# Query projections of one head and four tiles in the first attention layer of a fused transformer kernel

## The reference

```
q = (latents @ Wq).reshape(b, q_len, N_KV_HEADS, N_GROUPS, HEAD_DIM)      # 16 x 64 rows, 32 heads of 128
k = (hidden_states @ Wk)...   v = (hidden_states @ Wv)...                # context and latents, 4 kv heads
scores = einsum('bqhgd,bkhd->bhgqk', q, k) / sqrt(HEAD_DIM)               # 64 x 128 per head
out = softmax(scores) @ v ;  return out @ Wo                             # then x = x + out, layer norm
```

## Time and profile before

| what | value |
|---|---|
| median of three runs | 1513.99 us |
| profiled execution: time, span of its instructions | 1514.85 us, 1513.1 us |
| mean granted TensorE clock | 0.992 |
| PE, PEld, DVE, ACT, POOL busy | 97%, 87%, 68%, 61%, 27% |
| first attention | about 12 to 625 us of the span |

### The profile page before, as it was taken

One profiled execution on the slowest core, in us unless ns is written; L12 is line 12 of the kernel. 1 busy time (PEld: TensorE's weight loads), 2 busy tenths in 40 slices (PEclk: granted clock), 3 DMA queues, 4 the chain that ended last, 5 costly groups with the idle time before them and its releaser, 6 DMA issues.

```text
span 1513.1 us, 27936 instructions
## 1 busy us (share of the span) xinstructions
PE 1472.1 (97%) x9532; PEld 1316.5 (87%) x9532; DVE 1032.4 (68%) x2449; ACT 926.9 (61%) x3133; POOL 402.4 (27%) x461
## 2 busy tenths in 40 slices
PE   8999999999999999998999999999999999989997
PEld 7999999999999998887888888888888888877885
DVE  7556555655565557886777777777777788767776
ACT  4456455545564555547777777777777774466652
POOL 5112011301130102233232323232323242644431
PEclk9999999999999999999999999999999999989999
DMA  5000100010000100101111110101010101011101
GB/s 219 33 29 29 43 29 29 29 43 29 29 29 29 43 29 27 57 35 43 36 43 42 37 50 29 50 29 50 29 50 29 39 8 67 29 46 37 48 15 60
DMA packets 16115, 62.60 MB, mean 41 GB/s; under 512 B 2228, under 2 KB 3764, under 8 KB 10984
## 3 DMA queue, kind: packets, MB, share of 16 engines
q1 hardware_dynamic: 15976, 60.82, 11.5%
HBM read 58.72 MB, written 2.10 MB: 40 GB/s over the span
## 4 chain that ended last, share of the span: by engine, by line
PE 54%; issue 26%; DVE 9%; ACT 6%; POOL 4%; DMA 0%; SPq 0%; POOLq 0%; ACTq 0%; DVEq 0%
PE psY L958 12%; PE psQ L874 9%; PE psKV L898 7%; PE psSO L843 2%; PE psSO L945 2%; POOL wo L541 2%; PE psTP L859 2%; PE psTP L908 2%; PE psQ L859 1%; PE psQ L799 1%; PE psSO L844 1%; PE psTP L928 1%; PE psKV L814 1%; ACT prob L1487 1%; PE psQ L1245 1%
## 5 line engine op out<-in xcount | busy, mean ns | idle before, releaser
L958 PE MATMUL psY<-wo,oT 128*128 128x512 f32 x1536 | 378.2, 394 | 0.7 <-DVE oT L1943 0.2
L958 PEld LDWEIGHTS psY<-wo,oT 128*128 128x128 f32 x1536 | 278.8, 188 | 56.2 <-POOL wo L541 2.2
L541 POOL TENSOR_TENSOR wo<-stage_o,wo 128x512 fp32r<-128x512 f32 x68 | 87.2, 1313 | 310.3 <-ACT wo L1400 279.6
L1400 ACT ACTIVATE pT<-psTP 64x256 fp32r<-64x256 f32 (+1 forms) x192 | 86.5, 451 | 124.2 <-PE psTP L928 123.4
L1490 ACT ACTIVATE prob<-wide,neg_mx 128x128 f32<-128x128 f32 x256 | 99.7, 391 | 81.5 <-DVE neg_mx L2075 81.5
L1487 ACT ACTIVATE prob<-s_sb,neg_mx 128x64 f32<-128x64 f32 x256 | 85.9, 337 | 94.2 <-DVE neg_mx L2075 94.2
L1943 DVE TENSOR_TENSOR pT<-psTP,pT 64x256 fp32r<-64x256 f32 (+1 forms) x192 | 97.6, 508 | 67.3 <-ACT pT L1400 65.5
L665 POOL TENSOR_TENSOR rms<-ms_eps,minus_half 128x5 f32<-128x5 f32 (+1 forms) x64 | 74.2, 1159 | 230.6 <-DVE ms_eps L2088 229.8
L541 POOL TENSOR_TENSOR wq<-stage_q,wq 128x512 fp32r<-128x512 f32 x42 | 53.9, 1301 | 209.3 <-ACT wq L1400 156.6
L898 PEld LDWEIGHTS psKV<-wkv,arena 128*128 128x128 f32 x768 | 100.3, 190 | 6.8 <-DVE kT L2123 1.8
L874 PE MATMUL psQ<-wq,hT 128*128 128x512 f32 x384 | 103.8, 407 | 0.0
(11 more groups left out here) (329 smaller groups left out, 3489.9 us busy)
## 6 DMA issues: line engine op xcount, KB each, us to landing
stage_o<-in_wo SPq DMA_DIRECT2D x16, 1024.0 KB, 4.8
stage_q<-in_wq SPq DMA_DIRECT2D x15, 1024.0 KB, 5.1
stage_kv<-in_wkv SPq DMA_DIRECT2D x12, 512.0 KB, 3.6
stage_q<-in_ctx SPq DMA_DIRECT2D x16, 256.0 KB, 3.0
stage_o<-in_ctxT SPq DMA_DIRECT2D x2, 1024.0 KB, 4.8
stage_q<-in_base SPq DMA_DIRECT2D x2, 1024.0 KB, 4.9
stage_kv<-in_ctx SPq DMA_DIRECT2D x8, 256.0 KB, 3.0
out<-x_res SPq DMA_DIRECT2D x8, 256.0 KB, 2.2
```

The lines of the kernel that those rows point to most:

```text
L541: g.tensor_tensor(dst[LO], stage, dst[HI].bitcast(f32), ALU.subtract).then_inc(ld[done or what + "_lo"], 1)
L958: m = mm(psY[:], oT[:, ol, h, :], wo[:, wl, h, :], start=h == 0 and i == 0, stop=h == HQ - 1 and i == 2)
L1400: copy = lambda o, i: nc.scalar.activation(o, i, ACT.Copy)
```

## The change

In head groups 1 to 6 a unit is one head for four tiles: 4 slices x 3 passes = 12 matmuls of 512 columns (`lat_four`). Groups 0 and 7 keep the units of two heads and two tiles. A query buffer `heads_of_four` of 16 KB per partition takes the place of kT1, v1, qT and xn; it holds four tiles' heads and is refilled in place. Its upper end is shared with xn, so that some norms (`alone`) go to q_sb, a single buffer. PE computes units earlier: unit t + 3 in step t, reached by two units each in steps 4 and 6; no unit stands in steps 53 and 54. ACT and DVE copy two units in every even step of groups 1 to 6, one before `exps` / `normalise` and one after, and none in odd steps. The splits of Wq move to steps 5, 12, 20, ..., 52, those of Wk and Wv to 14, 30 and 46. `ln_norm` of the next block goes behind `row_max` in steps 60 to 62.

```diff
+    at_top = nc.sbuf_top // 32 * 32 - 16384
+    heads_of_four = nc.alloc_sbuf_tensor_at("heads_of_four", [P, 4096], f32r, offset=at_top)
+    xn = nc.alloc_sbuf_tensor_at("xn", [P, 2, D], f32, offset=at_top + 12288)
...
+    pairs = heads_of_four[:].rearrange("p (l m h t) -> p l m h t", l=2, m=16, h=2)
...
+    def lat_four(hl, k, first):
+        return hT[:, hl, k, first:first + 4, 1:3].rearrange("p n b t -> p n (b t)")
...
-    def units_of(st):
-
-        first = [st] if st.static and st.t == 0 else []
-        return first + [st.back(-1)] * st.back(-1).exists
+    def units_of(t):
+
+        early = {0: (0, 1), 1: (2,), 2: (3,), 3: (4,), 4: (5, 6), 5: (7,), 6: (8, 9), 7: (10,), 8: (11,)}
+        if t.t > STEPS - NT - 4:
+            return [unit(t.t + 1)] if STEPS - NT <= t.t + 1 < STEPS else []
+        return [unit(k) for k in early.get(t.t, (t.t + 3,))]
+
+    def units_kept(t):
+
+        early = {0: (0, 1), 1: (), 2: (2, 3), 3: (4,), 4: (5, 6), 5: (7,)}
+        if t.t > STEPS - NT - 4:
+            return units_of(t)
+        return [unit(k) for k in early.get(t.t, () if t.t % 2 else (t.t + 2, t.t + 3))]
...
+    def changes_wq(t):
+
+        return t.exists and t.t in (5, 12, 20, 28, 36, 44, 52)
...
             def q_unit(k):
 
                 need(pe, s["qT_lo"], k.t - 1)
...
+                else:
+                    parts = [(unit_bank(k)[:].rearrange("p (n t) -> p n t", n=4), k.t % 4)]
+                for out, h in parts:
+                    head = slice(h * HD, (h + 1) * HD)
                     for c in range(KT):
                         if k.res(NT) == 0 and h == 0:
                             wq_split(k.div(NT) + a.wq0, c, True)
+                        tokens = (lambda xl: lat_pair(xl, c, k.res(NT) // 2)) if by_pairs(k) else (
+                            lambda xl: lat_four(xl, c, k.t // 4 % 2 * 4))
...
-                units = [] if a.rms else units_of(t)
-                scores_first = not a.rms and not units
+                units = [] if a.rms else units_kept(t)
+                scores_first = not a.rms and t.t >= STEPS - 1
...
                 if t1.exists:
                     exps(t1)
+                for k in units[1:]:
+                    unit_hi(k)
...
-                if a.norm_slot(t):
+                if a.norm_slot(t) and (a.rms or scores_first):
                     ln_norm(next_ln, t.t - LN_SLOT)
...
                     row_max(t1)
-                for k in units[-1:]:
+                if a.norm_slot(t) and not a.rms and not scores_first:
+                    ln_norm(next_ln, t.t - LN_SLOT)
+                for k in units[:1]:
                     unit_lo(k)
...
                 if t1.exists:
                     normalise(t1)
+                for k in units[1:]:
+                    unit_lo(k)
```

More of the change, by code:

```diff
@@ L304, in norms_of, with alone, xn_of @@
         return [0, 1] if t == 4 else [t - 3]
-    def xn_slot(ln, n):
-        return {5: 1, 6: 0, 7: 0}.get(ln, n % 2)
+    def alone(ln, n):
+        return ln == 0 and n > 5 or ln == 1 and n < 5
+    def xn_of(ln, n):
+        return q_sb[:] if alone(ln, n) else xn[:, {5: 1, 6: 0, 7: 0}.get(ln, n % 2)]
     def ln_bank(ln, n):
@@ L1002, in attention @@
                         kv_proj(t)
-                    if t1.exists and units:
+                    if t1.exists and not ending:
                         scores(t1)
@@ L1569, in attention @@
                     squares(t)
-                changes_wq = not a.rms and t.exists and t.res(8) == 6 and t.t < LN_SLOT
-                if changes_wq:
+                new_wq = not a.rms and changes_wq(t)
+                if new_wq:
                     next_wq(t, 0, 1)
@@ L1579, in attention @@
                     squares(t)
-                for k in units[:-1]:
-                    unit_hi(k)
+                if t.t == 0 and units:
+                    unit_hi(units.pop(0))
                 if a.index == 0 and t.static and t.t == 0:
@@ L1602, in attention @@
                     next_wq1(t)
-                if changes_wq and not early:
+                if new_wq and not early:
                     next_wq(t, 2, 3)
@@ L2202, in attention @@
                     gates(FF[1], 0)
-                for k in units[:-1]:
-                    unit_lo(k)
+                if t.t == 0 and units:
+                    unit_lo(units.pop(0))
                 between = first if t.static and t.t == 0 else ()
@@ L2228, in attention @@
                     k_normalise(t)
-                if t.exists and not a.rms and t.res(8) == 6 and t.t < LN_SLOT:
+                if not a.rms and changes_wq(t):
                     low_wq(t.div(8) + 1, 3)
```

93 lines of the change are left out of this document (57 added, 36 removed).

## The result

The changed kernel takes 1519.68 us (median of 20 runs, 1517.52 to 1522.95) against 1514.82 us of the kernel before (median of 20 runs too): ratio 1.0033, 95% interval 1.0026 to 1.0039. It is 4.9 us slower, which is real but far inside 2%. Two of the 20 runs of the kernel before, 3684.55 and 1607.56 us, stand far outside the others, and the median hardly feels them. The forecast was 1517.6 (1511.5 to 1524). The profiled execution is the slowest of the 20, 1522.95 us with a span of 1521.2, so its last microseconds need care.

What follows compares the result with a forecast made beforehand. PE, busy 97% at full clock, was taken to bound the kernel. The terms -3.4 + 4.8 + 0.8 + 3.0 - 1.0 - 0.6 gave +3.6 us on the profiled 1514.85; median forecast 1517.6 us, range 1511.5 to 1524.

Steps and rivals of the forecast that it cites:

- The units: Query units of groups 1 to 6: 12 wide matmuls take 2.81 instead of 2.88 us, 3.4 us saved over 48.
- the first rival: Units cost 2.74 us and the Wo splits catch up: gain without the losses, 1512.8 us; chance 18%.
- Steps 53 and 54: Steps without a unit: transposes wait for the division, kv_proj for the low part of k; 4.8 us lost.
- The opening: Unit 4 in the first steps waits for unit 2's copy, moved from step 1 to 2; 0.8 us lost.
- The clock plays no part: First attention: stalls under 3 us each at full clock, so no clock cost was counted.
- Wo: Six steps splitting Wo (10, 18, 26, 34, 42, 50): second copy delays what PE needs, 0.5 us each, 3.0 lost.
- Wq: Three reloads outside kv steps: the unit's wait for DVE's Wq slice goes; 1.0 us saved over three.
- The norm: Steps 60 to 63, norm behind the maxima: 1.2 us gained, 0.6 paid in steps 60 to 62, net 0.6 saved.
- The second: Rival: margin in kv steps is used up, 11 even kv steps wait 0.3 us each; 1523 us; chance 15%.
- the 0.2 us of margin: Even kv steps: room left before kv_proj waits for the low part of k, so nothing is lost there.
- the third: Rival: single query buffer stalls every pair of steps, slower by over 2%, from 1545 us; chance 2%.
- the fourth: Rival: weight loads set the units' pace, 67 us saved, 1450 us, faster by over 2%; chance 1%.

Runs made afterwards that it cites:

- second profile: A second profile of the same changed kernel, unaltered, taken beside the profiled run of 1521.2 us span: span 1518.4 us.
- experiment 1: Changed kernel with each four-tile unit made as two halves of 12 matmuls of 256 columns: 1525.97 us, 1.0073 to the kernel before.
- experiment 4: Changed kernel with the two steps without a unit at 56 and 62 instead of 53 and 54: 1519.18 us, 1.0024 to the kernel before.
- Experiments 5 and 8: Changed kernel, second unit copy at step's end: in every such step, 1518.21 us (5); only where Wo splits and step 52, unit 2 copied in step 1, 1515.39 us (8).
- Experiments 10 and 11: Experiment 9 plus first DVE unit copy ahead of the maxima: in all steps splitting Wq, 1514.34 us (10); in steps 12, 28, 44 alone, 1513.51 us (11).
- Experiment 9: Changed kernel with unit 2 copied in step 1, second copy late only where Wo is split, empty steps at 56 and 62: 1514.79 us, 0.9999.
- experiment 3: Changed kernel with 16 unread identity matmuls of 128 columns before unit 4, where PE waits: 1520.55 us, 1.0033 to the kernel before.

## Why the prediction was right, and which terms were not

The sum was +3.6 and the median came out at +4.9; sign, size and class were right, and the time was 2.1 us off. The sign rests on mechanisms that held: the lost cover in steps 53 and 54 and the copies in front of Wo cost more than the wider matmuls give. That the figure came so near is partly luck: against the forecast the units gave 3.8 us more, while the clock in the opening (+1.5), Wq (+1.4), Wo (+0.7), the norm (+0.5) and the rest of the kernel (+1.2) took 5.3 more (second profile).

- **The units: mis-sized.** The step took 2.81 us "since it is the same stage with the same stationary width". The trace has 2.75, the figure of the later dense product, and experiment 1 ties 0.14 us a step to it: 7.2 saved instead of 3.4, or 5.4 net. The column count and the width were right; what 2.81 holds besides is the slow first step of a batch that stands behind narrow matmuls, which the units do not. The row for the right price was in the trace of the kernel before, the output product at 628.48, so "all output products of this stage that do not wait look like 2.81", said against the first rival, had an exception.
- **Steps 53 and 54: right.** +4.9 against +4.8, with the two named waits, 1.53 and 0.88 in step 53, 1.32 and 0.28 in 54; experiment 4 moves them with the empty step.
- **The opening: wait right, its consequence missed.** The wait is worth 0.85 us for 0.8 forecast. The text before had said "The clock plays no part: the stalls below are under 3 us each in a stage that runs at full clock." That is the failed sentence: behind stalls of 0.7 to 2 us the granted clock fell in several executions, for about 1.5 us each.
- **Wo: right in size, half right in mechanism.** 3 x 0.5 + 3 x 0.64 + 2 x 0.15 = 3.7 for 3.0. In kv steps the wait is that of psKV on the low part of k, as forecast, against the earlier trace rows. Outside them it is not POOL's slice that comes first but oT, whose high part stands behind the added copy on ACT; POOL's old wait is still there behind it, not longer than before (1.9 us in four waits against 2.2, where 1.1 instead of 0.6 had been forecast for three). Experiments 5 and 8 take the added waits away. The changed kernel's rows, PE at the output product of step 11, its weight loads there, and PE at the keys and values of step 19:

```profile
136.29 3.10 PE L1012 MATMUL psY<-wo,oT 128*128 128x512 f32 x11 [0.33 <-DVE oT L1999]
...
138.64 0.53 PEld L1012 LDWEIGHTS psY<-wo,oT 128*128 128x128 f32 x3 [0.47 <-POOL wo L589]
...
207.00 2.18 PE L952 MATMUL psKV<-wkv,hT 128*128 128x256 f32 x16 [0.49 <-DVE arena L1999]
```

- **Wq: wrong sign.** The old wait went (-0.53 each), oT did not give any of it back, but "Units 5, 6 and 7 find their banks free" had been checked in the opening only. Later, unit 16 needs the bank of unit 14 one step after that unit's copy, and the copy is late where the negated maximum takes 0.83 us instead of 0.17. +0.65 each, so 0.4 us lost over three where 1.0 was to be saved. Experiments 10 and 11 show that the place of the copy decides: ahead of the maxima it frees the bank in time.
- **The norm: gain right, price too low.** 1.15 gained for 1.2 forecast; 0.3 + 0.3 + 0.42 paid for 0.6, as the price of step 64 had not been counted. The norm now stands behind the negated maximum (DVE), and the transposes of the norm (PE) start at its end, while the output product had been through some 0.25 earlier, at 605.84 + 2.81 = 608.65:

```profile
608.30 0.55 DVE L2039 TENSOR_SCALAR q_sb<-x_res,mv,rstd 128x512 f32<-128x512 f32 x1
...
608.90 0.66 PE L833 MATMUL psKV<-ident,q_sb 128*128 128x128 f32 x4
```

Of the rivals, the first (units at 2.74) had the units right and the Wo splits wrong: they did not catch up. The second did not occur: ordinary kv steps keep their 0.15, so the 0.2 us of margin sufficed. Nothing came near the third or the fourth.

## What to carry to other kernels

Price a merged instruction by rows of its shape that stand behind the same kind of batch, and look at the starts of its single matmuls: 2.75 and 2.81 us differed by the first step alone. When copies are bunched in every second step, check each step type (reload, kv, group border) for who stands behind the copy and for the age of the bank it frees, and place the copy by type: late everywhere gained 3.9 us and lost 3.7, late only where Wo is split gained 2.9 and lost 0.6. A wait that is cured by moving work may have been the sign of something else: here the wait on Wq went and one on a bank came, both behind the same slow operation. A stall of more than a microsecond on a saturated PE may have a second price, the clock behind it, which is paid in some executions only.

## What the runs showed of the hardware

**At times PE runs at half clock behind a short stall.** The changed kernel's profiled run has four such stretches up to 1308 us (columns as above), one of them shown above, these the others:

```profile
20.00:28.00 8.00, 4.94 (x27) 0.79 0.37 131
700.00:708.00 8.00, 5.75 (x22) 0.79 0.02 9
1268.00:1276.00 8.00, 7.27 (x37) 0.79 0.62 229
```

The kernel before has one, after a wait of 1.6 us for q_sb:

```profile
692.00:700.00 8.00, 5.96 (x23) 0.79 0.15 61
```

and it has 1.00 at the other three places, although the stall before 1268 us (0.67 us, on POOL's part of Wk and Wv) is in it too. Experiment 9 has none, and the shortest span, 1510.6; experiment 10, with the same edits and one more, has them behind the wait of step 56 (4 us at 0.71) and at 692, and a span of 1513.5. The fourteen profiles give a count for each place (what PE waited, and in how many profiles it ran at the lower level behind it):

| place | wait of PE | lower clock behind it |
|---|---|---|
| before the first keys and values, 21 us | 2.2 to 3.2 us | 3 of 4 |
| the same | 0.4 to 1.0 us | 0 of 10 |
| unit 4, with unit 2 copied in step 2 | 1.9 us | 2 of 6 |
| step 53 without a unit | 1.5 us, then 0.3 or 0.9 | 3 of 8 |
| step 56 without a unit | 1.3 us | 2 of 5 |

Each costs about 1.5 us: the keys and values of step 53 take 4.6 instead of 3.1 us, the output product of step 56 takes 4.55 instead of 2.97. The Trainium skill, TensorE: Matmul & The Clock Gate, section Part 1: The HAM clock gate, says of a kernel's start that the same kernel differs from run to run in how many matmuls run slow, since the chip's watch runs free of the kernel; these profiles show such a difference from run to run in mid-kernel too. That the stall before was the cause in each case is argued from its place and from these counts, not shown: experiment 3 was the test of it, and it was inconclusive.

**VectorE's small operation waits for POOL's.** The negated maximum (128 x 4) takes 0.17 us. In all 105 places of the fourteen traces where it starts more than 0.04 us before the end of a POOL product (1.3 us each), it ends 0.02 to 0.03 us behind the end of that product, and so takes 0.30 to 1.11 us. The rows above show it: POOL's row ends at 143.82 + 3.81 = 147.63, the negated maximum at 146.83 + 0.83 = 147.66. VectorE's larger operations, on 512 columns, take 0.66 to 0.69 us beside POOL as without it. In experiment 10 the negated maximum comes later in POOL's last product, and takes 0.35.
